# Who takes the low half of the gathered rows: an expert stage with its subtraction moved from TensorE to GpSimd

## The reference

```
h = layernorm(x)                                  # 896 tokens, 512 channels
probs = softmax(h @ Wr)                           # 8 experts
w, idx = top_k(probs, 2); w = w / sum(w)
for e in range(8):                                # F = 512
    inner = silu(h @ Wg[e]) * (h @ Wu[e])
    output += w_e * (inner @ Wd[e])
x = x + tanh(g_ffn) * output
```

## Time and profile before

| | |
|---|---|
| median of 3 runs | 1136.43 us (1136.09 to 1137.81) |
| the profiled execution | 1136.88 us |
| its span, first to last instruction | 1134.8 us |
| granted TensorE clock, mean | 0.983 |
| busy, TensorE / VectorE / ScalarE / GpSimd | 1083.7 / 777.6 / 699.5 / 522.4 us |

### The profile page before, as it was taken

The page is one execution under the profiler, slowest core; times in us unless marked ns, Lnnn a source line. Parts: engine busy times, 40 slices in busy tenths (PEclk is TensorE's granted clock), DMA queues, the critical chain, the costliest instruction groups (busy, mean ns, idle before and its releaser), DMA issues. The chain is left out here.

```text
span 1134.8 us, 19580 instructions
## 1 busy us (share of the span) xinstructions
PE 1083.7 (95%) x5681; PEld 893.9 (79%) x5681; DVE 777.6 (69%) x1569; ACT 699.5 (62%) x2035; POOL 522.4 (46%) x601
## 2 busy tenths in 40 slices
PE   4599999999999999999999999998999789999996
PEld 3488888888888888888888888887888667777885
DVE  7999986977776897777697766668554884755000
ACT  7668888766888856888867656774241333443442
POOL 6756564445445454545544554452000235656432
PEclk8899999999999999999999999999999889999999
DMA  7221111152111114111114111111954356673310
GB/s 268 97 80 54 45 46 36 37 192 64 37 36 53 55 36 184 50 49 37 45 36 144 56 45 37 44 37 65 378 161 155 131 181 207 185 234 92 55 42 0
DMA packets 52819, 107.39 MB, mean 95 GB/s; under 512 B 6064, under 2 KB 27056, under 8 KB 51184
## 3 DMA queue, kind: packets, MB, share of 16 engines
q1 hardware_dynamic: 48016, 97.00, 25.9%
q0 software_dynamic: 4704, 9.18, 3.5%
HBM read 91.48 MB, written 16.52 MB: 95 GB/s over the span
## 5 line engine op out<-in xcount | busy, mean ns | idle before, releaser
L556 POOL TENSOR_TENSOR c_lo<-c_raw,c_hi 128x500 fp32r<-128x500 f32 x96 | 124.3, 1295 | 184.4 <-ACT c_hi L615 162.7
L534 POOL TENSOR_TENSOR rs<-va,mhalf 125x2 f32<-125x2 f32 (+1 forms) x180 | 202.5, 1125 | 14.1
L527 POOL TENSOR_TENSOR va<-ss,epst 125x2 f32<-125x2 f32 (+1 forms) x180 | 57.1, 317 | 160.3 <-DVE ss L1134 99.9
L834 PE MATMUL bank<-w_hi,c_hi 128*125 128x512 f32 x384 | 120.0, 434 | 7.8 <-ACT w_hi L610 6.2
L807 PE MATMUL bank<-w_hi,xqs 128*128 128x512 f32 (+2 forms) x464 | 110.2, 359 | 10.5 <-DVE xqs L1126 10.5
L834 PE MATMUL bank<-w_hi,c_lo 128*125 128x512 f32 x384 | 105.1, 395 | 0.0
L834 PE MATMUL bank<-w_lo,c_hi 128*125 128x512 f32 x384 | 105.0, 395 | 0.0
L698 ACT ACTIVATE work<-bank,nmax 112x375 f32<-112x375 f32 x128 | 73.6, 586 | 44.3 <-DVE nmax L1163 44.0
L807 PE MATMUL bank<-w_lo,xqs 128*128 128x512 f32 (+2 forms) x464 | 100.6, 339 | 0.1
L878 PE MATMUL bank<-kxT,qxT 128*112 128x375 f32 x256 | 96.9, 480 | 0.0
L834 PEld LDWEIGHTS bank<-w_hi,c_hi 128*125 128x125 f32 x384 | 67.0, 188 | 26.0 <-issue 6.4
(11 more groups left out here) (284 smaller groups left out, 2822.7 us busy)
## 6 DMA issues: line engine op xcount, KB each, us to landing
c_raw<-in_ctxT SPq DMA_DIRECT2D x96, 250.0 KB, 2.7
shared<-in_w_in SPq DMA_DIRECT2D x13, 1024.0 KB, 8.6
shared<-in_wproj SPq DMA_DIRECT2D x32, 256.0 KB, 4.7
raw_g<-in_Wg SPq DMA_DIRECT2D x8, 1024.0 KB, 6.5
raw_u<-in_Wu SPq DMA_DIRECT2D x8, 1024.0 KB, 7.1
raw_d<-in_Wd SPq DMA_DIRECT2D x8, 1024.0 KB, 5.4
cat_scratch<-results SPq DMA_DIRECT2D x32, 224.0 KB, 2.0
shared<-cat_scratch SPq DMA_DIRECT2D x2, 1792.0 KB, 10.4
```

The costliest lines, as they stand in the source:

```text
L527: pool.tensor_tensor(va[0:rows, lo:hi], ss[0:rows, lo:hi], epst[0:rows, lo:hi], ALU.add).then_inc(va_done, 1)
L534: pool.tensor_tensor(rs[0:rows, lo:hi], va[0:rows, lo:hi], mhalf[0:rows, lo:hi], ALU.pow).then_inc(rs_done, 1)
L556: pool.tensor_tensor(flat(c_lo[:, k, :, :]), flat(c_raw[:, k, :, :]), flat(c_hi[:, k, :, :]).bitcast(F32), ALU.subtract).then_inc(cl_done, 1)
L834: m = pe.matmul(bank[0:CT, :], a[:, ch, k, :], w[:, k, CKX:CV], start=(i == 0), stop=(i == 3 * KB - 1))
```

## The change

The low half of the rows is no longer made by a matmul. ScalarE copies `p_x` twice, rounded to `xh` and whole back over the gathered rows in `xr`, and GpSimd subtracts one from the other. The subtraction of the inner values stays as it was. GpSimd's order per tile becomes product, subtraction for the next tile, gather, add. The gate and up products are ordered so that the four blocks of high x high and the four of high x low come first; the wait for `xl` stands ahead of the last four. The gate products wait for `xh` only. The read of the table stands ahead of the up products, and the down products are in one piece. Of the lane comparisons, ScalarE makes the last six (as Relu(1 - |lane - value|)), VectorE eight and GpSimd none.

```diff
-    LP = 4
+    LA = 6
 # GpSimd
         def gather(i):
             if i >= 3:
-                pool.wait_ge(tx_rdy, i - 2)
+                pool.wait_ge(xl_done, i - 2)
...
+        def rows_low(i):
+            pool.wait_ge(xh_done, i + 1)
+            pool.wait_ge(xw_done, i + 1)
+            if i >= 2:
+                pool.wait_ge(u_rdy, i - 1)
+            pool.tensor_tensor(xl[:, i % 2, :], xr[:, i % 3, :], xh[:, i % 2, :].bitcast(F32),
+                               ALU.subtract).then_inc(xl_done, 1)
...
-        pool.wait_ge(lane_rdy, 1)
-        pool.wait_ge(cr_done, M)
-        for n in range(CH - LP, CH):
-            last = pool.tensor_scalar(lane_hot[:, n, :], lane_bf[:, :], lane_f[:, n:n + 1], None, ALU.is_equal)
-        last.then_inc(hot_done, 1)
...
         for i in range(3):
             gather(i)
+        rows_low(0)
...
         for i in range(TI):
             product(i)
+            if i + 1 < TI:
+                rows_low(i + 1)
+            if i + 3 < TI:
+                gather(i + 3)
             if i >= 1:
                 add(i - 1)
-            if i + 3 < TI:
-                gather(i + 3)
 # ScalarE
+        act.wait_ge(lane_rdy, 1)
+        for n in range(CH - LA, CH):
+            last = act.activation(lane_hot[:, n, :], lane_bf[:, :], ACT.Abs, bias=lane_f[:, n:n + 1], scale=-1.0)
+        last.then_inc(far_done, 1)
+        act.wait_ge(far_done, 1)
+        act.activation(lane_hot[:, CH - LA:, :], lane_hot[:, CH - LA:, :], ACT.Relu, bias=1.0,
+                       scale=-1.0).then_inc(hot_done, 1)
...
-        def rows_low(i):
-            act.wait_ge(sx_rdy, i + 1)
-            act.activation(xl[:, i % 2, :], p_x[:, :], ACT.Copy).then_inc(xl_done, 1)
+        def rows_whole(i):
+            act.activation(xr[:, i % 3, :], p_x[:, :], ACT.Copy).then_inc(xw_done, 1)
 # TensorE
             if i >= 1:
-                pe.wait_ge(xl_done, i)
+                pe.wait_ge(xw_done, i)
             for k in range(KB):
-                mm = pe.matmul(p_x[:, k * P:(k + 1) * P], xr[:, i % 3, k * P:(k + 1) * P], ident[:, :],
-                               start=(k == 0), stop=False, is_transpose=True, skip_group_check=True)
+                mm = pe.transpose(p_x[:, k * P:(k + 1) * P], xr[:, i % 3, k * P:(k + 1) * P], ident[:, :])
             mm.then_inc(tx_rdy, 1)
-
-        def rest_of_rows(i):
-            pe.wait_ge(xh_done, i + 1)
-            pe.matmul(p_x[:, :], minus[:, :], xh[:, i % 2, :], start=False, stop=True,
-                      skip_group_check=True).then_inc(sx_rdy, 1)
...
+        def products_of_rows(bank, i, n):
+            a_hi, a_lo = xh[:, i % 2, :], xl[:, i % 2, :]
+            for m, (a, w) in enumerate(((a_hi, hi), (a_hi, lo), (a_lo, hi))):
+                if m == 2:
+                    pe.wait_ge(xl_done, i + 1)
+                for k in range(KB):
+                    mm = pe.matmul(bank[:, :], a[:, k * P:(k + 1) * P],
+                                   w[n][:, bass.ds(at[i] + k, 1), :].rearrange("p a f -> p (a f)"),
+                                   start=(k == 0 and m == 0), stop=(k == KB - 1 and m == 2))
+            return mm
...
-        rest_of_rows(0)
         for i in range(TI):
-            pe.wait_ge(xl_done, i + 1)
+            pe.wait_ge(xh_done, i + 1)
...
+            if i + 1 < TI:
+                at[i + 1], split[i + 1] = weights_of(i + 1)
             pe.wait_ge(l_done[1], split[i])
-            products(pu, xh[:, i % 2, :], xl[:, i % 2, :], 1, at[i], range(KB)).then_inc(u_rdy, 1)
+            products_of_rows(pu, i, 1).then_inc(u_rdy, 1)
...
-                products(pd, hh[:, :], hl[:, :], 2, at[i - 1], (0, 1))
-            if i + 1 < TI:
-                rest_of_rows(i + 1)
-                at[i + 1], split[i + 1] = weights_of(i + 1)
-            if i >= 1:
-                products(pd, hh[:, :], hl[:, :], 2, at.pop(i - 1), (2, 3)).then_inc(dn_rdy, 1)
+                products(pd, hh[:, :], hl[:, :], 2, at.pop(i - 1), range(KB)).then_inc(dn_rdy, 1)
             turn_inner(i)
 # VectorE
-            for n in range(CH - LP):
+            for n in range(CH - LA):
```

More of the change, by code:

```diff
@@ L1451, in projected_experts @@
     lane_rdy = sem(c, "lane_rdy")
+    far_done = sem(c, "far_done")
     hi_done = sem(c, "ph_done")
@@ L1485, in projected_experts @@
     xh_done = sem(c, "xh_done")
-    sx_rdy = sem(c, "sx_rdy2")
+    xw_done = sem(c, "xw_done")
     xl_done = sem(c, "xl_done")
@@ L1708, in _ @@
         rows_high(0)
-        rows_low(0)
+        rows_whole(0)
         for i in range(TI):
@@ L1716, in _ @@
                 rows_high(i + 1)
-                rows_low(i + 1)
+                rows_whole(i + 1)
             if 1 <= i < TI - 1:
@@ L1878, in _ @@
                 pe.wait_ge(sg_done, i)
-            products(pg, xh[:, i % 2, :], xl[:, i % 2, :], 0, at[i], range(KB)).then_inc(g_rdy, 1)
+            products_of_rows(pg, i, 0).then_inc(g_rdy, 1)
             if i == 0:
```

## The result

The median went from 1136.32 us (1136.09 to 1137.81, 4 runs) to **1129.79 us** (1129.34 to 1130.58, 4 runs): ratio 0.994, 95% interval 0.9923 to 0.9958. The forecast was 1129.1 in a range of 1127.9 to 1134.9. The profiled execution took 1129.68 us with a span of 1128.0, 6.8 less than before. The total came out within 0.7 us, but some of its terms did not.

The account below looks back on a forecast made before the run. TensorE, busy for 95% of the span, was taken as the bound. Terms 4.5 + 1.6 + 0.2 + 1.0 = 7.3 us took the median from 1136.43 to 1129.1 us, range 1127.9 to 1134.9.

Parts of the forecast that it names:

- The removed subtraction: Between the down products: 19 row-subtraction matmuls of 0.235 us leave TensorE, 4.5 us less.
- The moved read: TensorE's table read, moved ahead of the up products, costs the same 0.07 us; bounds 0 and 0.235.
- The entry: Entry into the experts: gate products start on `xh` alone, 1.4 us earlier; 1.6 us gained, ends 1.1 and 2.4.
- the extra 1.5: Entry, first gate products: up to 1.5 us more if they escape the half-clock window or the clock doesn't fall.
- The lanes: Lane comparisons before the experts: redistributed over ScalarE and VectorE, 0.2 us gained; ends +0.35 and -0.3.
- The splitting tile: Five tiles where VectorE splits weights: product goes ahead of the up-weight cast, 0.2 us waits vanish, 1.0 us less.
- the row of 0.11: Earlier trace: a product 0.11 us behind VectorE's subtraction went first; so 0.04 behind the cast was taken as first.
- rival A: Splitting tiles: product comes behind VectorE's cast, row subtraction behind VectorE's, `xl` 0.95 us late; 1134.1 us; chance 0.25.
- Rival B: Splitting tiles: product behind the cast, but GpSimd keeps the port for both instructions; 0.1 us lost each; 1129.6; chance 0.10.
- C: Splitting tiles: GpSimd's queue too full, late add delays the product, 2.3 us cost in each of five; 1140.9; chance 0.07.
- D: Removed matmul not felt: first gate products or the moved read stall TensorE as much; 1132.2 us; chance 0.08.

Follow-up runs that it names:

- read-moved run: The kernel before with only the read of the table moved ahead of the up products; 1135.14 us, ratio 0.9983.
- read-back run: The changed kernel with the read of the table put back between the two halves of the down products; 1127.89 us, ratio 0.9931.
- seven matmuls: The changed kernel with seven matmuls with unused results in TensorE's tile 0 wait for product 0; 1127.46 us, ratio 0.9915.
- product-late run: The changed kernel with a one-column ScalarE copy ahead of the up copy from tile 2 on, delaying GpSimd's product; 1135.76 us, ratio 0.9986.
- add-first run: The changed kernel with GpSimd's add put ahead of its gather again; 1132.3 us, ratio 0.9958.

## Why the prediction was right, and where it was not

- **The removed subtraction, 4.5 us.** Right. 18 tiles (2 to 19) at 0.235 are 4.2; the nineteenth, that of tile 1, is inside the net 1.3 below.
- **The moved read, same 0.07.** Mis-sized: in its new place it costs nothing. The lower bound of zero was the truth, and 18 x 0.09 = 1.6 us came on top. The read-moved run shows the 0.09, the read-back run that the new place isn't the cause.
- **The entry, 1.6 us.** The start came 1.2 us earlier, against 1.4. The clock didn't spare the gate products of tile 0 (4.4 us as before), so nothing of the extra 1.5 came. I had followed the entry as far as product 0 and priced its meeting with VectorE at 0.3. The meeting itself was of that size, and not new: product 0 took 1.55 us where an undisturbed one takes 1.28, and 1.56 before. The step that failed is that the sum ends there, at "gives about 0.3 of it away", and puts nothing for the clock behind the wait. That cost 1.3 net in tile 1: without the subtraction, two waits of 0.75 and 0.74 became one of 1.97, and behind it the clock was low. The seven matmuls show that the idle was needed for that. Whether it was its being in one piece, or its being 0.5 us longer in all, is not shown.
- **The lanes, 0.2 us.** 0.5. The comparisons took 1.86 where I had 2.0, the Relu 0.84 where I had 0.95. No table load stands between them in the trace; the Trainium skill ("ScalarE: Activation LUTs", Table sets) had said so.
- **The splitting tile, 1.0 us.** The outcome is right in all five: product 0.01 to 0.03 ahead of the cast, cast 2.35, GpSimd and VectorE in turns, no wait. The reason that I gave for a product slightly behind the cast, the row of 0.11, is refuted: 0.09 behind loses when no gather stands directly ahead. So the outcome was luck. Nothing was measured at the 0.04 behind that I forecast, but between 0.03 ahead (first) and 0.06 behind (second) the rule of the first comer gives rival A there. It didn't come to that because the product came 0.08 earlier than I had put it, the read having cost nothing.
- **Rival A** was the second case and ran once, in tile 2, for 1.0 us. Its price was right (0.95 each in the prediction, 1.0 measured here and 1.26 per tile in the product-late run), and the point from which it decides was nearer than the 0.1 to 0.2 later that I wrote: a product 0.05 later than my +6.98, and 0.13 later than the +6.90 of the changed kernel, was enough. It had its chance of 0.25 by the distance that I thought it had; by the true distance it deserved more.
- **Rival B**, GpSimd keeping the port for two instructions, is what the add-first run shows, but only behind a gather. **C** didn't come: the add ended at 949.67, +5.03. **D** was excluded by the windows.
- The sum: -0.5, -1.2, -5.9, -1.0, -0.4 of drift ahead of the change, +1.3, +1.0. Together that is -6.7. The read (1.6) and what the drift (0.4) and the lanes (0.3) gave beyond the forecast stood against the clock and tile 2 (2.3), the entry (0.4) and the nineteenth subtraction (0.2), which the net of tile 1 holds.

## What to carry to other kernels

When work is taken out of the middle of a stall, look at what the two halves become: a longer idle of TensorE can cost more at a lower clock behind it than the work itself, and a few matmuls with unused results in the gap give it back. Where two engines share a port, work out each one's start against the other's to the tenth of a microsecond, and treat a lead under 0.1 us as luck that a small edit can turn; here 0.12 us cost 1.26 us per tile. A row of who went first carries over only to a place with the same instruction directly ahead.

## What the runs showed of the hardware

- GpSimd and VectorE took turns at the ends of instructions when both had work: a product 0.01 to 0.05 us ahead was first, one 0.05 to 0.10 behind second. Behind a gather in whose last 0.1 us VectorE's subtraction was issued, GpSimd went on for one instruction (3.57 us for the subtraction instead of 2.29) or, with its row subtraction next in line, for two (4.80 us). A subtraction issued 0.84 us before the end of a gather took 2.29. Why it differs stays open.
- A wait of 1.97 us of TensorE was followed by a granted clock of 0.50 (1.2 GHz), and 4.65 us for a stretch that takes 3.11 at 1.00, in an execution whose tile 0 had run at 0.62, and alike in four more profiles; with seven matmuls in the wait (tile 0 at 0.60) it was not.
- A register read on TensorE cost 0.09 us directly behind the subtraction of the rows, and nothing ahead of the up products or between two down products.
